# Maximum stage of a causal attention beside an fp4 gated layer: difference and score products on two halves of TensorE's rows, one reduction per block of queries

## The reference

```
def _L0_attn_ref(x, Wqkv, Wout, bout):
    qkv = x @ Wqkv.T
    q, k, v = jnp.split(qkv, 3, axis=-1)
    ...
    dots = jnp.einsum('bhid,bhjd->bhij', q, k) * scale
    causal_mask = jnp.triu(jnp.ones((t, t), dtype=bool), 1)
    dots = jnp.where(causal_mask, -jnp.inf, dots)
    attn = jax.nn.softmax(dots, axis=-1)
    out = jnp.einsum('bhij,bhjd->bhid', attn, v)
    ...
x = L0_attn_x
xn = _layernorm(x, axis=-1)
x = x + _L0_attn_ref(xn, ...) + _L0_ffn_ref(xn, ...)
```

## Time and profile before

| | us |
|---|---|
| median of 3 runs | 2459.28 (2459.23 to 2459.46) |
| the profiled execution, its own time | 2462.13 |
| its span | 2460.3 |
| projection's last VectorE operation ends | 195.9 |
| maximum stage: first product, first reduction | 218.5, 220.4 |
| maximum stage: last reduction, last transpose | 928.3, 929.0 |
| mean granted TensorE clock | 0.987 of full |

### The profile page before, as it was taken

One profiled execution on the slowest core, in us unless ns is written; L12 is line 12 of the kernel. 1 busy time (PEld: TensorE's weight loads), 2 busy tenths in 40 slices (PEclk: granted clock), 3 DMA queues, 4 the chain that ended last, 5 costly groups with the idle time before them and its releaser, 6 DMA issues.

```text
span 2460.3 us, 85898 instructions
## 1 busy us (share of the span) xinstructions
PE 2295.5 (93%) x34104; PEld 1274.1 (52%) x34104; DVE 2032.9 (83%) x5926; ACT 1952.6 (79%) x3342; POOL 666.0 (27%) x530
## 2 busy tenths in 40 slices
PE   5995999999999998999999999999999999999998
PEld 4883444444444444555555555555555555555555
DVE  5977999999999997778877787777787777778776
ACT  2445999999999997888877788877788877878875
POOL 2324344244333422222222222221212212122221
PEclk8997999999999999999999999999999999999999
DMA  5665455444554461101201111111011022011000
GB/s 151 210 216 87 68 79 78 70 67 74 78 76 67 68 110 33 30 16 32 64 24 39 31 33 30 59 31 38 22 41 32 18 66 45 19 41 32 14 21 32
DMA packets 94544, 143.91 MB, mean 58 GB/s; under 512 B 24896, under 2 KB 73920, under 8 KB 93632
## 3 DMA queue, kind: packets, MB, share of 16 engines
q1 hardware_dynamic: 89792, 129.50, 26.2%
q0 software_dynamic: 4352, 8.92, 1.5%
HBM read 104.20 MB, written 34.14 MB: 56 GB/s over the span
## 4 chain that ended last, share of the span: by engine, by line
PE 47%; issue 6%; ACT 6%; DVE 3%; POOL 0%; DVEq 0%; ACTq 0%; POOLq 0%
PE O L1168 16%; PE F L1189 10%; PE S L1147 10%; ACT probs L1298 6%; PE F L1226 5%; PE F L1235 2%; PE F L1215 2%; PE S L1153 1%; DVE o_turned L1491 1%; DVE o_turned L1492 0%; PE S L1235 0%; PE F L1182 0%; DVE o_sum L1496 0%; DVE xt_lo L1441 0%; DVE o_packed L1503 0%
## 5 line engine op out<-in xcount | busy, mean ns | idle before, releaser
L1298 ACT ACTIVATE probs<-S 128x1024 f32<-128x1024 f32 (+3 forms) x1280 | 1077.3, 897 | 233.2 <-PE S L1153 129.6
L924 ACT ACTIVATE m_excess<-m_DIFF 128x512 f32<-128x512 f32 (+7 forms) x1536 | 647.4, 473 | 84.3 <-PE m_DIFF L884 39.0
L942 DVE CUSTOM_DVE_ANT_0 m_excess<-m_S,m_excess 128x512 f32<-128x512 f32 (+7 forms) x1536 | 700.7, 530 | 11.9 <-PE m_S L884 9.7
L1168 PE MATMUL O<-probs,v_sb 64*32 64x512 f32 (+3 forms) x10240 | 613.2, 532 | 1.0 <-ACT probs L1298 1.0
L882 PE MATMUL m_S<-m_k,m_q 128*128 128x512 f16 (+7 forms) x1536 | 482.7, 324 | 26.8 <-DVE m_row_max L942 17.4
L882 PE MATMUL m_DIFF<-m_k,m_q_diff 128*128 128x512 f16 (+7 forms) x1536 | 477.6, 318 | 25.7 <-DMA m_q_diff<-s_q 25.4
L1147 PE MATMUL S<-q_st,k_st 64*32 64x512 f16 (+3 forms) x10240 | 407.6, 350 | 61.2 <-ACT probs L1298 49.5
L1147 PEld LDWEIGHTS S<-q_st,k_st 64*32 64x32 f16 x10240 | 146.6, 90 | 391.2 <-ACT probs L1298 258.9
L835 POOL TENSOR_TENSOR m_q_diff<-m_zero,m_q 48x4096 f16<-48x4096 f16 x32 | 224.4, 7013 | 414.8 <-DMA m_q<-s_q 400.4
L1362 POOL TENSOR_TENSOR h_norm<-gated,h_rscale 128x704 f32<-128x704 f32 x64 | 89.0, 1391 | 806.2 <-DVE h_rscale L1415 806.2
L882 PEld LDWEIGHTS m_S<-m_k,m_q 128*128 128x128 f16 x1536 | 148.2, 96 | 276.2 <-DVE m_row_max L942 195.3
(11 more groups left out here) (190 smaller groups left out, 3901.8 us busy)
## 6 DMA issues: line engine op xcount, KB each, us to landing
m_q<-s_q SPq DMA_DIRECT2D x96, 128.0 KB, 3.7
m_k<-s_k SPq DMA_DIRECT2D x96, 128.0 KB, 6.6
m_q_diff<-s_q SPq DMA_DIRECT2D x96, 128.0 KB, 7.9
k_st<-s_k SPq DMA_DIRECT2D x96, 128.0 KB, 4.4
q_st<-s_q SPq DMA_DIRECT2D x384, 32.0 KB
m_k<-s_k SPq DMA_DIRECT2D x96, 124.0 KB, 5.1
a_x<-in_L_attn_x_dram POOLq DMA_DIRECT2D x16, 512.0 KB, 5.2
s_q<-a_part SPq DMA_DIRECT2D x32, 256.0 KB, 2.5
```

Source lines behind the costliest of these rows:

```text
L924: act.activation(excess[u % MAX_EXCESS][:, 0:keys // 2], DIFF[u % MAX_BUFS][:, 0:keys // 2], ACT.Relu) \
L942: dve.tensor_tensor_reduce(larger, S[u % MAX_BUFS][:, 0:keys // 2], larger, 1.0, -3e38, ALU.add, ALU.max, column).then_inc(reduced[u % MAX ...
L1168: ins = pe.matmul(O[e][s * SLOT:(s + 1) * SLOT, st.skip:QC], v_sb[st.group % 2][rows, st.j, s * SLOT:(s + 1) * SLOT], probs[s // 2][st.n % ...
L1298: act.activation(probs[half][st.n % PROBS][:, :, 0:st.width], S[half][:, :, 0:st.width], ACT.Exp, scale=scale).then_inc(exped[half], 1)
```

## The change

Four things, in the words of the code:

1. **Row halves.** The stacks are 2 x 64 rows. Rows 0 to 63 hold queries and keys for S; rows 64 to 127 hold the same queries and **stored key differences** (odd run minus even run) for DIFF. Both products take 64 rows, and TensorE's list alternates between DIFF of the next unit and S of this one, piece by piece; the masks of both come last. There are no negated queries, and POOL has nothing to make in the stage.
2. **Whole rows as units.** A unit is a whole block of up to 1,024 columns, so a head has 16 units. DIFF and S have two buffers of two banks each; the four pairs of the narrowest blocks share a buffer. The order in a head is 15, 8, 7, 0, 6, 1, 14, 9, 13, 10, 5, 2, 4, 3, 12, 11. `MAX_LEAD` is 1, `m_excess` has six tiles of 1,024 columns. Both waits of a step stand ahead of its first product: `exceeded` of the unit that last held the banks of the next DIFF, and `reduced` of the one that last held the banks of this S. Rounds no longer drain TensorE's list, and the join (L946) is gone.
3. **Differences in the projection.** For each group ScalarE copies the keys to SBUF once more (a fifth copy of 1,024 columns), POOL makes the differences and their two parts (three operations of 512 columns), and SP stores them (two DMAs more). The next group's key products wait for that copy.
4. **First stacks early.** POOL zeroes the slots of the stacks in the weights stage and early in the projection and makes the masks there; SP loads the first two sets of stacks (12 DMAs each) in groups 7 and 9 of the projection.

The diff, cut to its core:

```diff
@@ projection_phase, POOL
+            def key_differences(r, p):
+                blocks = k_whole[p][:, :, :].rearrange("p o (n e k) -> p (o n) e k", e=2, k=PAIR)
+                ...
+                pool.tensor_tensor(k_diff..., blocks[:, :, 1, :], blocks[:, :, 0, :], ALU.subtract).then_inc(k_differenced[p], 1)
+                ...
+                pool.tensor_copy(diff_part[0][p][:, :, :], k_diff[:, :, :]).then_inc(diff_part0[p], 1)
+                pool.wait_ge(diff_part0[p], r + 1 + PRIMED)
+                pool.tensor_tensor(diff_part[1][p][:, :, :], k_diff[:, :, :], diff_part[0][p][:, :, :], ALU.subtract) \
+                    .then_inc(diff_part1[p], 1)
@@ projection_phase, TensorE, ScalarE, SP
+                    if h == 1:
+                        pe.wait_ge(k_copied[before[1]], before[0] + 1 + PRIMED)
+                act.wait_ge(part1_done[1][p], r + 1 + PRIMED)
+                act.wait_ge(k_differenced[p], r + PRIMED)
+                act.activation(k_whole[p][:, :, :], QK[:, 2:4, :], ACT.Copy).then_inc(k_copied[p], 1)
+                if g:
+                    store_differences(*later(r, p, -1))
+                if g in FIRST_LOADS_IN:
+                    ...
+                    stacks.load(sp, 0, FIRST_LOADS_IN.index(g), dram)
@@ units
-MAX_KEYS = 1024
-MAX_BUFS = 4
-MAX_EXCESS = 8
-MAX_LEAD = 2
+MAX_COLS = T // 2
+MAX_HALF = MAX_COLS // 2
+MAX_EXCESS = 6
+MAX_LEAD = 1
+    wide = [(i, NKB + NKB // 2 - 1 - i) for i in range(NKB - 1, NKB - NKB // 4 - 1, -1)]
+    narrow = [(i, NKB // 2 - 1 - i) for i in range(NKB // 2 - 1, NKB // 4 - 1, -1)]
+    for n, pair in enumerate(wide):
+        units += [MaxUnit(i, buf, 0) for buf, i in enumerate(pair)]
+        if n % 2 == 0:
+            units += [MaxUnit(i, buf, at) for buf in range(2) for at, i in zip((0, MAX_HALF), narrow[n + buf])]
@@ shift_phase, TensorE
+                if lead:
+                    difference_ready(*lead)
+                if at:
+                    pe.wait_ge(reduced, holders(*at) + PRIMED)
+                for c in range(max(len(lead_cuts), len(cuts))):
+                    if c < len(lead_cuts):
+                        difference(*lead, *lead_cuts[c])
+                    if c < len(cuts):
+                        score(*at, *cuts[c])
+                if lead:
+                    masks(DIFF, round_units[lead[1]][1], slice(PAIR, P), differed)
+                if at:
+                    masks(S, round_units[at[1]][1], slice(0, PAIR), scored)
@@ shift_phase, VectorE
-            for p in range(2):
-                for stack in (q_diff[p], q_st[p], k_st[p]):
-                    dve.memset(stack[:, :, :].bitcast(F32), 0.0).then_inc(zeroed[p], 1)
```

More of the change, by code:

```diff
@@ L418, in _ @@
             over_groups(body)
+            key_differences(*later(0, 0, groups - 1))
         @block.vector
@@ L760, in load_first, with shift_phase @@
         self.load_tile(sp, 1)
-def shift_phase(nc, once, loop_sems, ident, dram, ahead, last_shift):
+def shift_phase(nc, once, loop_sems, dram, ahead, last_shift, stacks, ident):
     units = max_units()
-    assert len(units) % MAX_EXCESS == 0 and MAX_HEADS * NKB == P
-    split = MAX_KEYS // P
+    assert sorted(unit.block for unit in units) == list(range(NKB)) and MAX_HEADS * NKB == P
     primed = []
@@ L810, in loads_before, with before, holders @@
             return n * (loads // 2) + load // 2
-        round_units = [(h, *unit) for h in range(MAX_HEADS) for unit in units]
-        def uses(n, u, bufs):
-            return n * (len(round_units) // bufs) + u // bufs + 1
+        round_units = [(h, unit) for h in range(MAX_HEADS) for unit in units]
+        total = B * rounds * len(round_units)
+        def before(n, u):
+            return n * len(round_units) + u
+        def holders(n, u):
+            banks = set(round_units[u][1].banks)
+            for back in range(1, len(units)):
+                if before(n, u) >= back and banks & set(round_units[u - back][1].banks):
+                    return before(n, u) - back + 1
+            return 0
@@ L889, in differences, with masks, difference_ready @@
+            def masks(out, unit, rows, done):
+                end = unit.at + unit.cols
+                pe.matmul(out[unit.buf][:, end - PAIR:end], masked[rows, :], future[rows, :],
+                          start=False, stop=True).then_inc(done, 1)
+            def difference_ready(n, u):
+                h, unit = round_units[u]
                 if u % per_load == 0:
                     load = h // MAX_LOAD
-                    pe.wait_ge(stack_ld[load % 2], loads_before(n, load) * (16 * load_dmas) + 16 * load_dmas + PRIMED)
@@ L904, in _ @@
[L904 to L913 removed]
+                    pe.wait_ge(stacks.ld[load % 2], (loads_before(n, load) + 1) * (16 * stacks.dmas))
@@ new lines, in _ @@
+            for n in range(B * rounds):
+                for u, (h, unit) in enumerate(round_units):
+                    larger = excess[before(n, u) % MAX_EXCESS][:, 0:unit.cols]
+                    dve.wait_ge(scored, before(n, u) + 1 + PRIMED)
+                    dve.wait_ge(exceeded, before(n, u) + 1 + PRIMED)
+                    dve.sem_inc(stack_free[h // MAX_LOAD % 2] if (u + 1) % per_load == 0 else aside, 1)
+                    dve.tensor_tensor_reduce(larger, S[unit.buf][:, unit.at:unit.at + unit.cols], larger, 1.0, -3e38,
+                                             ALU.add, ALU.max, row_max[:, h, unit.block:unit.block + 1]).then_inc(reduced, 1)
+                dve.wait_ge(reduced, before(n, len(round_units)) + PRIMED)
+                dve.wait_ge(negated, n + PRIMED)
+                dve.transpose(row_turned[:, :], row_max[:, :, :].rearrange("p h i -> p (h i)")).then_inc(turned, 1)
+                dve.wait_ge(turned, n + 1 + PRIMED)
@@ L1605, in bass_attention_beside_fp4_gated_layer @@
             wts["down_" + half] = sb("w_down_" + half, [P, ITILES, D], F32R)
+        shared = [sb(f"shared{n}", [P, 2 * T]) for n in range(2)]
+        stacks = MaxStacks(sem, shared)
+        stacks.allocate(nc, ctx, sem)
         with ExitStack() as first:
```

271 lines of the change are left out of this document (134 added, 137 removed).

## The result

| | before | changed |
|---|---|---|
| median | 2459.37 us (2459.23 to 2460.61) | 2638.01 us (2637.76 to 2639.75) |
| ratio, 95% interval | | 1.0727 (1.0708 to 1.0745) |
| span of the profiled execution | 2460.3 | 2638.0 |
| projection's last VectorE operation ends | 195.9 | 214.4 |
| first reduction | 220.4 | 218.1 |

The change costs 178.6 us. The range (2425 to 2590) doesn't hold that; the forecast was 2496 us, and the rival "the clock falls to half, all of the stage" was 2634. In the profiled executions the loss is: projection +18.5, start of the stage (3.7 us behind the projection in place of 24.5) -20.8, stage itself 886.9 against 708.3, +178.6, rest +1.4; together +177.7.

The account below looks back on a forecast made before the run. VectorE was taken to set the pace in the maximum stage. Hand-over +48, stage start -20 and projection +9 gave +37 us on a median of 2459.3, forecasting 2496 us, range 2425 to 2590.

Parts of the forecast that it names:

- the clock falls to half, all of the stage: Maximum stage: TensorE at half clock throughout, 2634 us; the clock rival, half or all of the stage, had 17%.
- Clock, "I cost this at nothing": Maximum stage: TensorE some 66% busy, set against 64% at clock 1.00 in the trace; cost nothing.
- one of the signs of being wrong: Maximum stage: a granted clock under 1.00 would show the forecast wrong.
- The rule weighed there: Skill's rule: TensorE micro-idling between groups of matmuls while cycling through PSUM goes back and forth between two clocks.
- Units: Maximum stage: 16 units a head for 24, 512 reductions fewer at 0.08 us each, saving 41 us.
- Hand-over chain, +48 us: Maximum stage: with two buffers VectorE idles 1.40 us a head at hand-overs; 756 us against 708.
- the chain at half clock: Maximum stage: the same hand-over times at 0.83 ns a column, 13.91 us a head, 894 us.
- The halves overlap: Maximum stage: DIFF and S run side by side; the rival of no overlap, 2560 us, had 6%.
- Start of the stage, -20 us: Stage's start: zeroing, DMAs and first landing go, first reduction at 200.6 instead of 220.36; bounds -20 to -10.
- Projection, +9 (0 to +33): Projection: ScalarE's copy about 1 us, POOL's operations delaying VectorE 5, early loads 3; together +9 us.
- The zeroing, which I set beside POOL's own waits: Weights stage and projection: POOL's zeroing, some 7 us in each of two places, beside waits of 14 and 6 us.
- Sum: Whole kernel: +48 - 20 + 9 = +37 us, a median of 2496 us; the forecast's chance was 44%.

Follow-up runs that it names:

- The whole-row run: Changed kernel with both products and their masks over all 128 rows, one product behind the other; 2588.75 us, ratio 1.0528.
- The old units with row halves: Changed kernel with the units of the kernel before: at most 512 columns, 24 a head, four buffers, DIFF two ahead; 2466.79 us, ratio 1.0034.

## Why the prediction was wrong, step by step

- **Clock, "I cost this at nothing": the step that failed.** It cost 887 - 756 = 131 us, by the chain. The argument was that 64% busy at a clock of 1.00 answers to 66% in the changed kernel. TensorE was busy 80%, at half the clock, at which a column takes twice as long; a granted clock under 1.00 is one of the signs of being wrong that the prediction named. Busy time was the wrong thing to compare: whole rows kept 1.00 at 76%, and one half of the rows had 0.50 at 94%. The rows are of products on 128 rows; the two to compare differ in the rows of the array, which I left out of the argument. The tiles of 64 rows stand among others in the main stage and could not show it either.
- The rule weighed there (the Trainium skill, "TensorE: Matmul & The Clock Gate", A second HAM failure mode: psum-queue depth-cycling) pointed to the right rival for another reason. Its picture is a clock that goes back and forth where TensorE pauses between groups of products. The whole-row run has the same cycle through PSUM, VectorE waits 128 us in it and TensorE is idle for 24 of 100 us, and it stays at 1.00; the changed kernel lies at 0.50 without going back and forth. The old units with row halves do go back and forth, so the picture is seen in one run, but not in the one that the rule was weighed for.
- **Units**: right. The reductions of 1,024 columns take 1.225 us, and VectorE is busy 706 us, as 512 reads fewer and the columns have it.
- **Hand-over chain, +48 us**: right as a mechanism, and to within about 2% in the three cases that ran (837, 887, 1143 us against 820, 894, 1142). Its own value at full clock, 756, was not seen. VectorE idles 177.6 us and not 90. ScalarE is what was waited for in half of it, 90.0 us, as said, but before 512 columns too: the waits before 960 and 832 alone are 58 of 158 us between 250 and 1,050 us, some 37%. And VectorE waits before blocks 11, 5 and 3, where the chain at full clock had nothing; the chain at half clock was not written out by block.
- **The halves overlap**: right.
- **Start of the stage, -20 us**: measured -20.8.
- **Projection, +9 (0 to +33)**: measured +18.5. POOL's differences cost 6.1 where I took 5; the loads 5.5 where I took 3. The zeroing, which I set beside POOL's own waits, costs some 6 (215.1 against 209.0 us with the old units): a wait of POOL is no cover if VectorE works in it. The clearings of 7.07 us lie beside VectorE's work on the weights (the projection starts 3.2 us later), those of 7.10 beside eight normalisations (6.2 us, and 2.9 before).
- Sum: +37 forecast; +178.6. The chance of 17% for the clock was too small, and the range should have reached its far end: the only argument against that rival was a stretch of 3.5 us.

## What to carry to other kernels

Splitting the array's rows to run two products side by side can halve TensorE's clock, and may then gain nothing: here whole rows, one product behind the other, were faster by 49 us. When a change lowers the rows that products use, compare the granted clock only with stretches of the same tile shape, and keep the rival of half clock for the whole stage inside the range. Where a reader of PSUM sets the pace, four small buffers with DIFF two units ahead absorbed the slower clock almost wholly (the stage was 8 us longer at a mean clock of 0.77, and 13 us at 0.50); two large ones did not.

Work on POOL is not free because POOL was idle: look at what VectorE does in that time.

## What the runs showed of the hardware that I had not expected

- The granted clock followed the rows of the products: 1.00 on 128 rows (busy 76 and 96 of 100 us), 0.50 on 64 rows (busy 80 side by side, 94 one behind the other), 0.77 and 0.50 on 64 and 48 rows in the flow of the old units. The rows alone don't decide, since 64 rows side by side gave both 0.50 and 0.77; and in the main stage products on tiles of 64 rows x 32 columns run at 1.00, beside others on 128 rows. In the kernel before, half of the rows of queries under S hold zeros, and the clock is 1.00. This suggests that the rows addressed count and not what stands in them; no run tests it.
- The drop from 1.00 came in the middle of the stage, 2.9 us behind the first product on half of the rows (637.11 and 640.0). The rise in the changed kernel came 12 us behind the last transpose.
- Changing between tiles of 64 and 128 rows cost about 0.08 us a step, 83 us in the stage.
- VectorE's SBUF-to-SBUF normalisation took longer beside POOL's operations, up to three times as long (4.06 against 1.37 us for four) and 719 against 407 ns in the mean; its operation that reads PSUM did not (1.21 us in both kernels).
